# Attention's output summed as 64 by 375 beside the queries, six groups of gathered rows taken inside attention, and tile 0's places in a PSUM bank

## The reference, cut to what matters

```python
# second layer, for each token: 8 heads of 16 picked rows of a table, then causal attention
kv_scores, indices = _pk(x, Wq_pk, pk_keys)                       # 16 of 4096 rows a head
k = jnp.einsum('bnhk,bnhkd->bnhd', kv_scores, keys_table[ind])
v = jnp.einsum('bnhk,bnhkd->bnhd', kv_scores, values_table[ind])
attn = jax.nn.softmax(jnp.where(causal, jnp.einsum('bihd,bjhd->bhij', q, k), neg), axis=-1)
out = jnp.einsum('bhij,bjhd->bhid', attn, v)                      # then @ Wo, summed over heads
# third layer: the gradient of sum(mean((lmm(x Wk) - x Wv)^2) * alr) over two layers of weights,
# summed over all sequences; then one step, and lmm(x Wq) with the new weights
```

## Time and profile before

| | us |
|---|---|
| median of 3 runs | 6795.9 (6795.37 to 6803.57) |
| profiled execution | 6795.46 |
| its span, first to last instruction | 6793.6 |
| PE busy | 5417.7 (80%) |
| POOL busy | 4478.9 (66%) |
| DVE busy | 3201.8 (47%) |
| ACT busy | 2089.3 (31%) |

### The profile page before, as it was taken

The page is one execution under the profiler, slowest core; times in us unless marked ns, Lnnn a source line. Parts: engine busy times, 40 slices in busy tenths (PEclk is TensorE's granted clock), DMA queues, the critical chain, the costliest instruction groups (busy, mean ns, idle before and its releaser), DMA issues.

```text
span 6793.6 us, 88054 instructions
## 1 busy us (share of the span) xinstructions
PE 5417.7 (80%) x24336; PEld 3758.2 (55%) x24336; DVE 3201.8 (47%) x14095; ACT 2089.3 (31%) x4501; POOL 4478.9 (66%) x4574
## 2 busy tenths in 40 slices
PE   2668788887978878787878878787788878788867
PEld 1446556555656556565655656565565656555533
DVE  6534644544464453445454344545534454640156
ACT  0224233332423332232323223232323324232332
POOL 2676767767676776767677676767677676767300
PEclk9667677766767776676777677676767767676767
DMA  1211111111111111111111111111111111111000
GB/s 44 73 51 47 53 45 53 52 46 51 43 53 44 53 52 48 51 44 53 43 53 49 48 53 44 53 43 53 46 51 53 43 53 45 52 47 53 24 22 12
DMA packets 166417, 321.92 MB, mean 47 GB/s; under 512 B 81980, under 2 KB 90772, under 8 KB 165710
## 3 DMA queue, kind: packets, MB, share of 16 engines
q0 software_dynamic: 144384, 295.20, 15.1%
q1 hardware_dynamic: 21166, 20.00, 1.1%
q10 hardware_dynamic: 288, 0.07, 0.0%
HBM read 310.37 MB, written 4.61 MB: 46 GB/s over the span
## 4 chain that ended last, share of the span: by engine, by line
POOL 34%; PE 29%; DVE 15%; issue 15%; ACT 4%; DMA 3%; DVEq 0%; POOLq 0%; SPq 0%; ACTq 0%
POOL store L427 34%; PE gath L613 9%; DMA store<-in,idx_now 3%; PE accu L475 2%; PE dense L467 2%; PE work L636 2%; DVE mx L1359 2%; PE gath L663 1%; PE sims L655 1%; DVE idxf L1299 1%; DVE picks L1295 1%; PE work L595 1%; PE work L690 1%; DVE prob_odd L1356 1%; PE work L648 1%
## 5 line engine op out<-in xcount | busy, mean ns | idle before, releaser
L427 POOL DMA_INDIRECT store<-in,idx_now x4512 | 4457.6, 988 | 1773.8 <-issue 1349.3
L613 PEld LDWEIGHTS gath<-wbd,store 128*128 128x128 f32 (+1 forms) x9024 | 1598.1, 272 | 804.1 <-issue 658.5
L613 PE MATMUL gath<-wbd,store 128*128 128x8 f32 (+1 forms) x9024 | 1591.1, 314 | 508.2 <-DMA store<-in,idx_now 500.1
L887 ACT ACTIVATE past<-dense,edge 128x375 bf16<-128x375 f32 x1024 | 588.2, 574 | 1613.7 <-PE dense L462 1613.4
L475 PE MATMUL accu<-dense_w,store 128*128 128x375 f32 x2048 | 1029.0, 591 | 33.0 <-ACT dense_w L895 33.0
L467 PE MATMUL dense<-parts_f,hot 128*128 128x375 bf16 x3072 | 819.5, 384 | 47.4 <-ACT dense_w L895 45.1
L895 ACT ACTIVATE dense_w<-dense 128x375 f32<-128x375 f32 x1024 | 495.5, 484 | 275.4 <-PE dense L468 260.2
L475 PEld LDWEIGHTS accu<-dense_w,store 128*128 128x128 f32 x2048 | 455.0, 237 | 136.8 <-issue 91.8
L467 PEld LDWEIGHTS dense<-parts_f,hot 128*128 128x128 bf16 x3072 | 317.7, 109 | 366.9 <-issue 274.0
L462 PE MATMUL dense<-ranksT,hot 128*128 128x375 bf16 x1008 | 379.6, 377 | 70.5 <-ACT past L887 70.3
L468 PE MATMUL dense<-past,far 128*128 128x375 bf16 x1024 | 397.6, 388 | 0.0
(11 more groups left out here) (276 smaller groups left out, 6685.3 us busy)
## 6 DMA issues: line engine op xcount, KB each, us to landing
store<-in,idx_now POOLq DMA_INDIRECT x4512, 2.5
x_in<-in SPq DMA_DIRECT2D x16, 187.5 KB
store<-in SPq DMA_DIRECT2D x1, 2048.0 KB, 8.9
queries_kept<-n3T SPq DMA_DIRECT2D x16, 93.8 KB, 2.3
h_saved<-h SPq DMA_DIRECT2D x16, 93.8 KB
store<-queries_kept SPq DMA_DIRECT2D x16, 93.8 KB, 2.3
store<-h_saved SPq DMA_DIRECT2D x16, 93.8 KB
out<-store SPq DMA_DIRECT2D x16, 93.8 KB
```

The costliest lines, as they stand in the source:

```text
L427: nc.gpsimd.indirect_dma_start(rows[0:slots, r * PER + i, :], None, kv_table, bass.IndirectOffsetOnAxis(ap=idx_now[0:slots, at:at + 1], ax ...
L613: last = mm(gath[:, 0, at:at + 8], rows[0:slots, r * PER + i, :], wbd[0:slots, t * GATHERS + n, :], start=True, stop=True)
L887: fn(past[:, n % 2, :], dense[:, 0, 0:S], ACT.Relu, bias=edge[:, 0:1]).then_inc(s["dense_u"], 1)
```

## The change

1. **Sum.** `mix` now makes the turned sum, 64 by 375, in `work[D:128, 0]`, the upper half of the bank in whose lower half the queries are made: 3 matmuls a head of 375, 250 and 125 columns, `vo` as the stationary side. After the last head ACT copies it to SBUF (`oT`), PE turns it back with 3 transposes into `work[:, 1]`, and DVE adds it from there. `gath` is free during attention. `turn_picks` of tile 2 now waits for that addition (`h2_done`), since it writes the same bank.
2. **Last outputs.** `last_outputs` uses `work[:, 1]` and stands behind `mix(h - 1)` at head h = 6; PE then waits for ACT's copy of it before the transposes of head 6, and ACT does that copy behind the exponentials of head 7.
3. **Groups.** Of the 36 groups six are taken in attention, one each at heads h = 2 to 7 (`GROUPS_INSIDE`), in the stretch between `queries(h + 2)` and the dense steps. They leave `FILL_PREPARE` (2), `FILL_GRADIENT` (3) and `FILL_SECOND` (1). ACT copies this first half at the start of `turn`. The first batch takes its six at the start of `turn(0)`.
4. **Places.** `gradient` no longer uses `sims[:, 0]`: its products go to the upper halves of `work` and to `work[:, 0]`. Tile 0's places lie in `sims[0:P, 0]`.

```diff
-FILL_PREPARE = ((2, 1), (1, 1), (2, 1), (1, 1), (2, 1), (1, 1), (2, 1), (1, 1), (2, 1))
+FILL_PREPARE = ((2, 1), (1, 1), (2, 1), (1, 1), (2, 1), (1, 1), (2, 1), (1, 0), (2, 0))
...
+GROUPS_INSIDE = (0, 0, 1, 1, 1, 1, 1, 1)
...
+        oT = two_q[D:128, 0:S]
...
-        place_banks = (places_s[:], sims[0:P, 0], places_s[:])
+        place_banks = (sims[0:P, 0], sims[0:P, 0], places_s[:])
...
@@ turn_picks, take_group (PE)
+                if t == 2:
+                    pe.wait_ge(s["h2_done"], b + 1)
...
-                if g == 0 and t == 0:
-                    pe.wait_ge(s["h2_done"], b + 1)
...
@@ attention (PE)
+            def take_inside(b, n):
+                for _ in range(n):
+                    take_group(b, 0, at_group[0])
+                    at_group[0] += 1
...
                 def mix(h):
                     pe.wait_ge(s["pT_done"], b * H + h + 1)
-                    if h == H - 1:
-                        pe.wait_ge(s["vo_done"], b * (NT + 1) + NT + 1)
-                    for c, (i, j, at) in enumerate(PAIRS):
-                        last = mm(gath[0:P, 0, i * D:(i + 1) * D], pT[:, c // 3, at:at + P], vo[:, j, h * D:(h + 1) * D],
-                                  start=(h == 0 and c == 0), stop=(h == H - 1 and c == 5), skip_group_check=True)
+                    for j in range(NT):
+                        last = mm(work[D:128, 0, j * P:S], vo[:, j, h * D:(h + 1) * D], pT[:, min(j, 1), (0, 0, 2 * P)[j]:(S, 2 * P, S)[j]],
+                                  start=(h == 0 and j == 0), stop=(h == H - 1 and j == NT - 1), skip_group_check=True)
...
-                    if h + 1 == H - 1:
-                        last_outputs()
                     if h + 2 < H:
                         queries(h + 2)
+                    if following:
+                        take_inside(b + 1, GROUPS_INSIDE[h])
                     dense_steps(b, STEPS_A[h])
                     if h >= 1:
                         mix(h - 1)
+                    if h + 1 == H - 1:
+                        last_outputs()
+                        pe.wait_ge(s["vo_done"], b * (NT + 1) + NT + 1)
                     pe.wait_ge(s["s_norm"], b * H + h + 1)
...
-                mix(H - 1).then_inc(s["o_mm"], 1)
+                mix(H - 1).then_inc(s["turned_mm"], 1)
+                pe.wait_ge(s["half_done"], b * (H + 1) + H + 1)
+                for t in range(NT):
+                    last = tr(work[0:P, 1, t * D:(t + 1) * D], oT[:, tile(t)], ident[D:128, D:128])
+                last.then_inc(s["o_mm"], 1)
...
@@ gradient (PE)
-                mm(sims[0:D, 0, 0:S], mlrb[:], n3T[:], start=True, stop=True).then_inc(s["x0_mm"], 1)
+                mm(work[D:128, 0, 0:S], mlrb[:], n3T[:], start=True, stop=True).then_inc(s["x0_mm"], 1)
...
-                mm(sims[0:D, 0, 0:S], w1T_s[:], dz[:, 1, :], start=True, stop=True).then_inc(s["dx_mm"], 1)
+                mm(work[D:128, 1, 0:S], w1T_s[:], dz[:, 1, :], start=True, stop=True).then_inc(s["dx_mm"], 1)
...
@@ attention, turn (ACT)
+                act.wait_ge(s["turned_mm"], b + 1)
+                nc.scalar.copy(oT, work[D:128, 0, 0:S]).then_inc(s["half_done"], 1)
...
             def turn(b):
+                fill(b, 0, sum(GROUPS_INSIDE))
                 keep_ranks(b)
```

More of the change, by code:

```diff
@@ L130, in tower @@
         mlrb = sb("mlrb", [D, D])
-        mblr_s = sb("mblr_s", [D, 1])
+        mblr_s = sb("mblr_s", [128, 1])
         params = sb("params", [D + 1, 2, D])
@@ L642, in last_outputs @@
                     for j in range(NT):
-                        last = mm(work[0:P, 0, j * D:(j + 1) * D], kvT[D:128, H - 1, tile(j)], wo_s[D:128, H - 1, :],
+                        last = mm(work[0:P, 1, j * D:(j + 1) * D], kvT[D:128, H - 1, tile(j)], wo_s[D:128, H - 1, :],
                                   start=True, stop=True)
@@ L721, in gradient @@
                     for t in range(NT):
-                        tr(sims[0:P, l, t * D:(t + 1) * D], (x0, x1)[l][0:D, tile(t)], ident[0:D, 0:D])
-                        last = tr(sims[0:P, l, 192 + t * D:192 + (t + 1) * D], dz[:, l, tile(t)], ident[0:D, 0:D])
+                        dst = (work[0:P, 0], sims[0:P, 1])[l]
+                        tr(dst[:, t * D:(t + 1) * D], (x0, x1)[l][0:D, tile(t)], ident[0:D, 0:D])
+                        last = tr(dst[:, 192 + t * D:192 + (t + 1) * D], dz[:, l, tile(t)], ident[0:D, 0:D])
                 last.then_inc(s["t_mm"], 1)
@@ L734, in turn @@
             def turn(b):
+                if isinstance(b, int) and b == 0:
+                    take_inside(0, sum(GROUPS_INSIDE))
                 turn_ranks(b)
@@ L1022, in attention @@
                         soften(*soften_next)
+                    if h + 1 == H - 1:
+                        act.wait_ge(s["vo_mm"], b * (NT + 1) + NT + 1)
+                        nc.scalar.copy(vo[:, :, (H - 1) * D:], work[0:P, 1, 0:NT * D].rearrange("p (j d) -> p j d", d=D)).then_inc(s["vo_done"], 1)
                     act.wait_ge(s["half_mm"], b * H + h + 1)
@@ L1041, in gradient @@
                 between()
-                fn(sg[:, 2, :], sims[0:D, 0, 0:S], ACT.Sigmoid, bias=mblr_s[:, 0:1]).then_inc(s["alr_done"], 1)
+                fn(sg[:, 2, :], work[D:128, 0, 0:S], ACT.Sigmoid, bias=mblr_s[D:128, 0:1]).then_inc(s["alr_done"], 1)
                 nc.scalar.copy(n3T[:], sims[0:D, 1, 0:S]).then_inc(s["mq_done"], 1)
@@ L1049, in gradient @@
                 act.wait_ge(s["t_mm"], b + 1)
-                for l in range(2):
-                    nc.scalar.copy(xt[:, l, :, 0:D], sims[0:P, l, 0:192].rearrange("p (t d) -> p t d", d=D))
-                    last = nc.scalar.copy(dzt[:, l, :, :], sims[0:P, l, 192:384].rearrange("p (t d) -> p t d", d=D))
+                for l, src in enumerate((work[0:P, 0], sims[0:P, 1])):
+                    nc.scalar.copy(xt[:, l, :, 0:D], src[:, 0:192].rearrange("p (t d) -> p t d", d=D))
+                    last = nc.scalar.copy(dzt[:, l, :, :], src[:, 192:384].rearrange("p (t d) -> p t d", d=D))
                 last.then_inc(s["t_done"], 1)
@@ L1415, in gradient @@
                 dve.wait_ge(s["dx_mm"], b + 1)
-                v.tensor_tensor(g2, g2, sims[0:D, 0, 0:S], ALU.add).then_inc(s["g1_done"], 1)
+                v.tensor_tensor(g2, g2, work[D:128, 1, 0:S], ALU.add).then_inc(s["g1_done"], 1)
                 dve.wait_ge(s["g1_done"], b + 1)
```

25 lines of the change are left out of this document (11 added, 14 removed).

## The result

The changed kernel takes 6382.0 us (median of 4 runs, 6375.2 to 6385.3) against 6799.7 us before (4 runs, 6795.4 to 6805.7): a ratio of 0.9376, 95% interval 0.9356 to 0.9396. It is faster. The forecast was 6400 us, in a range of 6365 to 6510.

A forecast was written before the change was run, and what follows sets the result against it. It took POOL and PE to wait for each other by turns, neither engine full; turns of 366 us for 392.9 save 377 us, with 20 + 5 - 3 outside 399, so 6396, said as 6400 us, range 6365 to 6510.

The forecast's parts named there:

- what is left is whichever of the two has more to do: Once POOL and PE stop waiting for each other by turns, the engine with more work sets the loop's turn.
- POOL's demand: POOL's own time in a turn of the loop: 392.9 - 24.6 - 5.0 + 1.0 = 364.3 us.
- The stall: POOL's long wait in attention for PE to take a group: goes whole, -24.6 us a turn.
- The places: Tile 0's places moved from SBUF to PSUM: gathers beside its picks no longer slowed, 5.0 us a batch.
- PE's demand: PE's time in a turn without waits for landings: 364.4 us before, 366.7 after, between 363 and 377.
- What is added: PE's extra time in attention: groups in heads 2 to 5 7.4 us, head 6 1, head 7 2, the end 2.4.
- What leaves: PE's groups gone from the stretches outside attention: -12.5 us a turn in all, 7.1 of it for groups at 3.53 us.
- rival B: PE becomes the bound with a demand of about 374 us, POOL waiting behind attention: 6510 us, chance 0.25.
- rival C: TensorE's clock falls in attention as thin matmuls break its rhythm, +32 us a turn: slower, 6880 us, chance 0.04.
- The sum: Whole-kernel total: turns of 366 us save 377 us, the parts outside the loop 20 + 5 - 3, together 399.
- D: PE waits in attention for groups not yet landed, losing what POOL gains: the same time, 6790 us, chance 0.03.
- E: The clock rises where PE no longer waits, and POOL's contention falls by 6.9: 6350 us, chance 0.06.

The follow-up runs named there:

- e1: The changed kernel with tile 0's places back in SBUF, all else as changed: 6463.2 us, ratio 0.9502 to the kernel before.
- r5: The changed kernel with a small memset on POOL and a wait for it ahead of every third group of gathers: 6479.6 us, ratio 0.9517.
- r8: The changed kernel with POOL's copy of the next tile's indices taken ahead of a tile's last group: 6346.4 us, ratio 0.9328.
- r6: The changed kernel with three more matmuls of 375 columns on PE in each of attention's 19 dense steps: 6393.9 us, ratio 0.9389.
- e3: The kernel before with only tile 0's places moved to PSUM and the gradient's products out of their bank: 6736.2 us, ratio 0.9898.
- e2: The changed kernel with no groups in attention, the six back in their earlier places: 6786.5 us, ratio 0.9958.
- r7: The changed kernel with six more matmuls of 375 columns on PE in each of attention's 19 dense steps: 6452.6 us, ratio 0.9474.
- e8: The changed kernel with the next tile's indices copied ahead of a tile's last group, on the slow chip: 9016.1 us, ratio 0.9709.
- e7: The changed kernel with six more matmuls in each of attention's 19 dense steps, on the slow chip: 9312.5 us, ratio 1.0039.

## Why the prediction was right

**The bound.** The step "what is left is whichever of the two has more to do" held. The turn is POOL's own time in three ways: its busy time and gaps add up to the turn, work added to it is seen whole (e1, r5), and work taken from it as well (r8); work added to PE is mostly not seen (r6).

**POOL's demand.** Forecast 392.9 - 24.6 - 5.0 + 1.0 = 364.3 us, measured 363.2. The stall is gone whole. The places gave 5.4 us by e1 and 5.0 by e3, put at 5.0. Tile 2's picks cost POOL what the forecast feared: a gather of 1.79 us beside `L1323`, where hardly any was issued before; what the gathers lose beside tile 2's picks is 4.0 us a turn before and 5.5 after, so 1.5 more, put at 1.

**PE's demand is the term that was mis-sized**, 366.7 us, with a measured 363.2 - 11.9 = 351.3. By the stretches of the windows, means over twelve turns:

| stretch | before | after | forecast | measured |
|---|---|---|---|---|
| attention | 100.0 | 112.8 | +12.8 | +12.8 |
| to the gradient's last products | 148.7 | 147.2 | -3.4 | -1.5 |
| the rest, less waits for landings | 115.6 | 91.4 | -7.1 | -24.2 |

What is added was right in sum, by luck in part, since it is made of four guesses: 7.4 + 1 + 2 + 2.4. In its rows PE's waits at the end are 0.74 and 0.76 us, with transposes of 0.51 us for the 0.96 assumed, and the seventh group's wait is 1.68 us for 2. e2 puts the sum and its links, without groups, at 4.5 us where 3.4 stood, and so the six groups at some 8 us, where 9.4 stood; that is the split that I can show. What leaves was priced as two groups at 3.53 us, 7.1, and 24 came. The other 17 us are the clock, by an estimate from the windows: PE's busy time times its clock is 37.67 x 0.66 + 75.89 x 0.69 = 77 us of full speed before and 27.54 x 0.87 + 63.98 x 0.80 = 75 after, so the work hardly shrank. The plainest part of it is the third window, in which PE has next to no gap in both kernels: 176 matmuls on record in 37.7 us at 0.66, and 160 in 28.2 us at 0.87. The 16 that are fewer are the group that left, 3.5 us; the other 6 us are the same work at a higher clock. (Over twelve turns it is less: 35.9 us at 0.70 and 28.2 at 0.86.) In the fourth window the clock went from 0.69 to 0.80, in the mean from 0.69 to 0.82. I had kept the clock of before for all that stays there, though I wrote under rival B that it would ease. The clock in attention did not fall with thin matmuls set into it, 0.82 in both windows and 0.79 and 0.81 in the mean: rival C is refuted.

Why the clock rises is shown for the last stretch, where it follows PE's waits for landings with PE's program unchanged (r8 to e1). In the stretch ahead of it PE waits for next to nothing in either kernel. There the clock is 0.66 in nine of twelve turns before, and 0.82 to 0.87 in every turn of each kernel that takes one group there instead of two; why is not shown.

**The sum.** Turns: I took 366 between 364.3 and 366.7, and it is 363.2. The 14 turns of the loop gave 403.2 us where 377 stood, and the last attention with a following batch 13.8 where 20 stood. Ahead of the first attention 5 us were to be won, and 3 were lost: that part holds the first batch's six groups at the start of `turn(0)`, and POOL waits 18.8 us for the first of them, 2.5 more than the 16.3 before. At the end 3.3 were lost, put at 3. 403.2 + 13.8 - 2.9 - 3.3 = 410.8, which is the difference of the two spans (6793.6 - 6382.8); the forecast was 399. That it is only 12 us off is partly luck: 26 us too little for the loop stand against 14 too much for the rest, and PE's demand, 15 us too high, did no harm only because it came out just 2.4 us above POOL's.

**The rivals.** B (6510) needed PE's demand at 374 and was given 0.25. Measured, PE had 12 us of waits left, and r6 took up 7.4 of its 8.4 added us with 7.9 us of waits still there; B's chance was too high, because it rested on a demand in which the clock was held fixed. r7 shows B's mechanism, a stall of POOL behind attention. It is real, but begins between the 8.4 us of added attention of r6, which cost 1.0 us, and the 15.6 of r7, which cost 4.8; the forecast had no air at all. D is refuted by e2 and by PE's waits for landings: none lies inside attention in the twelve turns, and a whole turn has 4, 11.5 us where 28.5 were. E (6350) named the clock and was right on that; it did not see that a faster PE gives nothing once POOL is the bound.

**What it said the profile would show.** POOL's total for PE under 60 us: 36.9. Tile 0's gathers at 0.94: so. PE's waits for landings under 10 us: 11.5, a miss that speaks for a PE with more air than thought. Attention longer by 10 to 15 us: 12.8. A turn of 364 to 368 us: 363.2, just under. A wait for ACT of about 2 us ahead of the seventh group: 1.68.

## What to carry to other kernels

When two engines wait for each other by turns, take out the longer wait, and compare what each has to do in a turn, gaps between its instructions counted: here POOL's busy share (66% before, 69% after) hid 0.30 us beside each of 282 gathers, and it was the bound at a turn of 363 us. An engine's demand that is read with its waits subtracted still holds the clock that those waits go with; price it at both levels of TensorE's clock, and call PE the bound only if its demand stays above the other engine's at the higher level too. Once an engine is the bound by its own stream, tenths of a microsecond in that stream are worth looking for (the copy taken early: 0.6% of the time).

## What the runs showed of the hardware that was not expected

- A whole chip can be 36% slower than others with the same kernel (9280 against 6806 us), with instructions on ACT and POOL that last as long as elsewhere. Waits on ACT that end with nothing in the profile, up to 30.4 us, come with it (in e8's trace). A verdict from such a chip can be another one than elsewhere: e7 takes 0.4% longer than the kernel before there (1.0039), and r7, the same kernel, is 5% faster on another chip (0.9474).
- A gather on POOL behind a semaphore that POOL itself has signalled starts 0.81 us after a memset and 0.97 us after a copy, against 0.30 us behind another gather. With a group of gathers between the copy and the wait for it (r8), 0.17 us behind the copy are left.
- PE's granted clock in one and the same stretch went from 0.66 to 0.87 in the turns shown (0.70 to 0.86 in the mean), with no edit to its work there but one group fewer. That was worth 6 us of the 37.7 in that turn, as much as three groups at the higher clock.
- An edit to POOL's stream alone moves PE's clock where PE waits for POOL: from 0.85 (r8) to 0.78 (e1) with the same PE program, 6 us of PE's time in the last stretch of a turn.
